# K's split turned in three products of sixteen rows per head, its diagonal tile filled by transfers that read each row twice, in an attention kernel on one Trainium2 core

## The chip, the core and the metric

The kernel runs on one core of a Trainium2 chip. Its engines are TensorE (PE: matrix products, with a row of its own, PEld, for loading weights), VectorE (DVE), ScalarE (ACT), GpSimd (POOL) and SyncE (SP). SP computes nothing here; it issues nearly all transfers, one after the other, and waits in between. The metric is the time of one execution on the device, in microseconds, of which the median of several runs is quoted.

## The reference

Cross attention with image tokens, for B = 16 sequences of S = 128 queries, C = 160 channels, H = 20 heads of D = 8. Each context has 124 text tokens and 4 image tokens of 256 features:

```python
q = heads(hidden_states @ W_q)
k_t = heads(text_ehs @ W_k);  v_t = heads(text_ehs @ W_v)
probs_t = softmax(einsum('bhsd,bhtd->bhst', q, k_t) * Dh ** -0.5)
text_out = einsum('bhst,bhtd->bhsd', probs_t, v_t)
k_ip = heads(ip_ehs @ W_k_ip);  v_ip = heads(ip_ehs @ W_v_ip)
attn_scores = einsum('bhsd,bhnd->bhsn', q, k_ip) * attn_scale
qsem = l2norm(einsum('bhst,bte->bhse', probs_t, text_ehs))
sem = einsum('bhse,bne->bhsn', qsem, l2norm(ip_ehs))
probs_ip = softmax(attn_scores + 0.5 * sem) * spatial_mask
ip_out = einsum('bhsn,bhnd->bhsd', probs_ip, v_ip)
out = (text_out + ip_out) @ W_out + b_out + residual
```

## The kernel before

**Windows and groups.** The program is a pipeline of 16 windows, one per sequence: four written out, ten in a loop of two at a time, two written out. A window has five groups (g = 0 to 4) of four heads. Every engine has its own list of instructions, in the order in which they are written, and semaphores tie them together. In window b, TensorE scores the groups of sequence b, turns the probabilities of two groups before (L934), multiplies those of three groups before with `main_rhs` (L952 and L954, called the mains here), and in between prepares sequence b + 1: at g = 0 the Gram matrix, V and K (L924) and q (L1024), at g = 1 the K products (L1031), at g = 2 the q products (L1039), at g = 4 the fifth group's (L1001, L1002). VectorE takes a maximum of each group's scores (L778) and norms of the mains (L713); ScalarE does the exponentials (L612), copies the turned probabilities to SBUF (L565) and makes the copies named below.

**The scores.** TensorE multiplies rounded float32 (fp32r) here. K and q are each split into a high part, written rounded by ScalarE (L581, L618), and the rest, written by VectorE (L784, L724). A head then has 32 columns: K as high, rest, high, rest and q as high, high, rest, rest, eight channels each, so that one product gives all four terms. Products with the identity turn four heads at a time into 128 rows. K's turned rows go from PSUM into `k_stack` (L600 for four groups, L591 for the fifth), and from there by transfers into `k_diag`, a tile that is zero but for its diagonal blocks: rows 32 j to 32 j + 31 of a group hold head j, in the columns of head j. With it one product of 512 columns (L984) scores four heads.

**The transfers of a window on SP** (L341 to L388), in this order: image-token rows of `k_split` for the next window, `ctxT_sb`, `xT_sb`, `xn_sb`, `vrep`; then, once `k_stack` is written, four transfers into `k_diag` for groups 0 to 3 (L373), one that repeats `g_stage` into `main_rhs` ten times (L378), once the fifth group's copies are made four more into `k_diag` (L383), and the store of a result (L388).

**`g_stage` is one buffer.** It holds the Gram matrix on its way to `main_rhs`, and ScalarE writes it at g = 0 only when the transfer of the window before has landed. In ScalarE's list the V copy, K's high part, that group's probabilities and everything later stand behind that write:

```python
wait(act, s_ctx_mm, b + 2)
wait(act, s_grep[p], 16 * (i + 1))
act.activation(g_stage[:, NIP:NIP + TOK], pa[:, 0:TOK], ACT.Copy)
```

The order of SP is fixed by lines 368 to 388; `s_kst03` counts L600 and `s_grep` the `main_rhs` transfers.

Of the kernel before, what the change touches and what calls it, by code (L numbers as in the profile page):

```python
# [24 lines left out]
F32 = mybir.dt.float32  # L25
F32R = mybir.dt.float32r
# [13 lines left out]
PG = HG // 2  # L40
NPAIR = H // 2
# [11 lines left out]
def xattn_program(nc, xT, xn, ctxT, ipT, ipn, smask, wq, wkv, wkvip, wout, ident, hmask, kip_d, vip_d, out):  # L53
    with ExitStack() as ctx:
# [48 lines left out]
        kip_split = sb("kip_split", [B * NIP, H, 2, 2, D])  # L103
# [72 lines left out]
        s_kd03 = two(sem, "s_kd03")  # L176
        s_kd4 = two(sem, "s_kd4")
# [28 lines left out]
        s_k0_mm = sem("s_k0_mm")  # L206
        s_k1_mm = sem("s_k1_mm")
# [106 lines left out]
        def _(sp):  # L314
# [17 lines left out]
            sp.dma_start(kip_d, kip_split[:, :, :, :, :].rearrange("t h c a d -> t (h c a d)")).then_inc(s_kip_out, 16)  # L332
# [7 lines left out]
            def window(b, p, i, w):  # L340
                n = 1 - p  # L341
                if has(w) and has(w, ahead=1) and w != 0:
# [4 lines left out]
                    wait(sp, s_kq4, b + 1)  # L347
                    sp.dma_start(k_split[T:TOK, :, :, :, :].rearrange("t h c a d -> t (h c a d)").bitcast(F32),
# [19 lines left out]
                if has(w, ahead=1):  # L368
# [160 lines left out]
        def _(act):  # L529
# [6 lines left out]
            act.activation(k_split[:, :, :, 0, :], doubled(probsT_ps[0][:, 0:C]), ACT.Copy).then_inc(s_khi, 1)  # L536
            act.wait_ge(s_q_mm, 1)
            act.activation(q_split[:, :, 0, :, :], doubled(probsT_ps[1][:, 0:C]), ACT.Copy).then_inc(s_qhi, 1)
            act.wait_ge(s_kT, 1)
            act.wait_ge(s_zeros[0], 1)  # L540
            for j in range(2):
                rows = slice(32 * j, 32 * j + 32)
                last = act.activation(k_diag[0][rows, 0:G - 1, j, :], pa[rows, :].rearrange("r (g t) -> r g t", t=TOK), ACT.Copy)
                if j == 0:
                    last.then_inc(s_kd03[0], 32)
                else:
                    last.then_inc(s_kst03, 1)
# [598 lines left out]
```

## Time and profile before

| | |
|---|---|
| median of 3 runs | 227.78 us (226.53 to 228.21) |
| profiled execution | 225.47 us, of which the span is 223.5 |
| TensorE busy | 210.6 us (94%), granted clock 0.992 |
| VectorE busy | 183.7 us (82%) |
| ScalarE busy | 172.7 us (77%) |
| GpSimd busy | 149.3 us (67%) |
| queue q1 (all of SP's transfers), share of 16 engines | 44.8% |

Durations come from the one profiled execution. Times in a row are counted from the start of its span. The profile lists a matrix product's own duration, though it overlaps its neighbours; what one adds is read from the chain of waits. "SPq" is SP's time for issuing a transfer, not the transfer; its landing is counted separately, from the start of the issue.

### The profile page before, as it was taken

How to read it: one execution, taken by the hardware profiler on the slowest of the kernel's cores; microseconds unless marked ns; L12 is line 12 of the kernel's file. 1: busy time of each engine (PE TensorE's matmuls, PEld its weight loads, DVE VectorE, ACT ScalarE, POOL GpSimd, SP SyncE). 2: the span in 40 equal slices, each digit the busy share in tenths (PEclk: the TensorE clock that was granted, in tenths of full speed). 3: DMA queues.
4: the chain of work that ended last, by engine and by line, in shares of the span. 5: the costliest groups of instructions: out<-in, count | busy, mean ns of one | idle time of the engine just before them, and what ended most of it. 6: DMA issues, size and time to landing. Idle time of an engine off the chain costs nothing.

```text
span 223.5 us, 6984 instructions
## 1 busy us (share of the span) xinstructions
PE 210.6 (94%) x1619; PEld 197.6 (88%) x1619; DVE 183.7 (82%) x1147; ACT 172.7 (77%) x569; POOL 149.3 (67%) x255
## 2 busy tenths in 40 slices
PE   8986859999999999999999999999999999998984
PEld 8876749999899999989999999999999999997973
DVE  4726529797988979697979899897979797999893
ACT  2608739897987979788888889697988888897831
POOL 2152301929688696959696977969696969698870
PEclk9996999999999999999999999999999999999999
DMA  5530553555462644565454647264545455461101
GB/s 137 110 121 18 115 148 72 146 142 155 128 164 70 193 112 124 147 158 149 135 155 121 181 103 198 76 181 109 153 123 158 148 144 149 105 167 32 47 1 44
DMA packets 47340, 27.60 MB, mean 123 GB/s; under 512 B 8513, under 2 KB 45538, under 8 KB 47322
## 3 DMA queue, kind: packets, MB, share of 16 engines
q1 hardware_dynamic: 46682, 26.96, 44.8%
q10 hardware_dynamic: 640, 0.43, 0.8%
q8 instruction: 7, 0.11, 0.2%
q14 instruction: 11, 0.09, 0.1%
HBM read 10.14 MB, written 1.52 MB: 52 GB/s over the span
## 4 chain that ended last, share of the span: by engine, by line
PE 68%; DVE 9%; DMA 8%; POOL 4%; issue 4%; ACT 3%; SPq 3%; DVEq 0%; POOLq 0%; ACTq 0%
PE main_ps L952 13%; PE main_ps L954 12%; PE probsT_ps L934 11%; DMA main_rhs<-g_stage 8%; PE pa L924 8%; PE score_ps L984 6%; PE pb L1012 4%; DVE junk L713 3%; PE pb L1024 3%; PE pa L1031 2%; PE main_ps L870 2%; PE pa L1039 2%; POOL rnorm L500 2%; SPq L373 1%; PE probsT_ps L865 1%
## 5 line engine op out<-in xcount | busy, mean ns | idle before, releaser
L612 ACT ACTIVATE probs<-score_ps,negmax 128x124 f32<-128x124 f32 x320 | 93.2, 411 | 1.1 <-DVE negmax L778 1.0
L713 DVE CUSTOM_DVE_ANT_0 junk<-main_ps,probs 128x124 f32<-128x124 f32 x320 | 77.8, 280 | 2.5 <-PE main_ps L954 2.0
L952 PE MATMUL main_ps<-main_rhs,probsT 124*128 124x137 f32 x320 | 64.8, 283 | 2.7 <-DVE small L715 2.7
L954 PE MATMUL main_ps<-main_rhs,probsT 124*128 124x137 f32 x320 | 63.3, 279 | 0.0
L500 POOL TENSOR_TENSOR rnorm<-clamped,exponent 128x20 f32<-128x20 f32 x15 | 53.2, 3544 | 1.2 <-DVE clamped L698 1.2
L778 DVE TENSOR_REDUCE negmax<-score_ps 128x4 f32<-128x496 f32 x80 | 53.1, 663 | 0.0
L952 PEld LDWEIGHTS main_ps<-main_rhs,probsT 124*128 124x128 f32 x320 | 48.9, 190 | 4.5 <-ACT probsT L565 2.0
L565 ACT ACTIVATE probsT<-probsT_ps 124x512 f32<-124x512 f32 x80 | 50.9, 636 | 2.5 <-PE probsT_ps L934 1.7
L934 PE MATMUL probsT_ps<-ident_sb,probs 128*124 128x128 f32 x320 | 49.0, 276 | 0.0
L954 PEld LDWEIGHTS main_ps<-main_rhs,probsT 124*128 124x128 f32 x320 | 48.7, 188 | 0.0
L934 PEld LDWEIGHTS probsT_ps<-ident_sb,probs 128*124 128x124 f32 x320 | 39.1, 141 | 5.3 <-issue 0.4
L984 PE MATMUL score_ps<-k_diag,q_stack 128*128 128x512 f32 x80 | 39.1, 489 | 1.0 <-DMA k_diag<-k_stack 1.0
L777 DVE COPY ip_score<-score_ps 128x16 f32<-128x16 f32 x80 | 13.3, 166 | 19.5 <-PE score_ps L984 19.5
L715 DVE COPY small<-main_ps 128x26 f32<-128x26 f32 x160 | 28.8, 180 | 0.1
L713 DVE DVE_READ_ACCUMULATOR2_ANT norm<- 128x1 f32 x320 | 26.6, 83 | 0.0
L478 POOL TENSOR_TENSOR ip_exp_half<-ip_exp 128x40 f32<-128x40 f32 x14 | 3.5, 252 | 25.1 <-ACT ip_exp L606 25.1
L576 ACT ACTIVATE g_stage<-pa 128x128 f32<-128x128 f32 x15 | 4.2, 278 | 20.5 <-DMA main_rhs<-g_stage 13.5
L303 POOL TENSOR_TENSOR ip_prod<-vrep,ip_probs 128x640 f32<-128x640 f32 x13 | 18.2, 1403 | 0.0
L924 PE MATMUL pa<-wkv_sb,ctxT_sb 128*128 128x160 f32 x112 | 17.5, 299 | 0.0
L984 PEld LDWEIGHTS score_ps<-k_diag,q_stack 128*128 128x128 f32 x80 | 15.4, 193 | 1.2 <-DMA k_diag<-k_stack 1.2
L600 ACT ACTIVATE k_stack<-pa 128x512 f32<-128x512 f32 x15 | 9.0, 598 | 9.4 <-PE pa L1031 9.3
L924 PEld LDWEIGHTS pa<-wkv_sb,ctxT_sb 128*128 128x128 f32 x112 | 15.7, 190 | 0.0
(165 smaller groups left out, 343.5 us busy)
## 6 DMA issues: line engine op xcount, KB each, us to landing
main_rhs<-g_stage SPq DMA_DIRECT2D x16, 660.0 KB, 4.2
vrep<-vip_d SPq DMA_DIRECT2D x13, 320.0 KB, 3.6
k_diag<-k_stack SPq DMA_DIRECT2D x60, 64.0 KB, 2.2
ctxT_sb<-ctxT SPq DMA_DIRECT2D x16, 124.0 KB, 2.7
xT_sb<-xT SPq DMA_DIRECT2D x16, 80.0 KB, 2.1
xn_sb<-xn SPq DMA_DIRECT2D x15, 80.0 KB, 2.0
out<-out_sb SPq DMA_DIRECT2D x15, 80.0 KB, 1.7
k_diag<-k_stack SPq DMA_DIRECT2D x60, 16.0 KB, 1.8
```

Source lines behind the costliest of these rows:

```text
L303: eng.tensor_tensor(ip_prod[:, :, :, :], vrep[n][:, :, :, :], ip_probs[:, :, :].rearrange("s h m -> s m h").unsqueeze(3).broadcast_to([S, ...
L500: pool.tensor_tensor(rnorm[:, :], clamped[:, :], exponent[:, :], ALU.pow).then_inc(s_rnorm, 1)
L565: act.activation(probsT[tp][:, :, :].rearrange("t h s -> t (h s)"), probsT_ps[tp][0:T, :], ACT.Copy).then_inc(s_probsT, 1)
L612: last = act.activation(probs[p][:, h, :], score_ps[(p * G + g) % 2][:, j * TOK:j * TOK + T], ACT.Exp, bias=negmax[p][:, h:h + 1])
L713: dve.tensor_tensor_reduce(junk[:, 2 * r + a, :], u, probs[wb][:, h, :], 1.0, 0.0, ALU.mult, ALU.add, norm2[wb][:, h:h + 1])
L715: dve.tensor_copy(small[wb][:, PG * gg + r, :], main_ps[r][:, T:T + SMALL]).then_inc(s_norm, 1)
L778: dve.tensor_reduce(negmax[p][:, HG * g:HG * g + HG], sc[:, :, 0:T], AX_X, ALU.max, negate=True).then_inc(s_max, 1)
L924: mm = pe.matmul(pa[:, lo:lo + width], ctxT_sb[n][:, c, :], r, start=(c == 0), stop=(c == EC - 1))
L934: mm = pe.transpose(probsT_ps[tp][0:T, j * S:(j + 1) * S], probs[tb][:, HG * tg + j, :], ident_sb[:, :])
L952: pe.matmul(main_ps[r][:, 0:MAIN], probsT[mp][:, 2 * r, :], blk[:, RW - MAIN:RW], start=True, stop=True)
L954: pe.matmul(main_ps[r][:, MAIN:2 * MAIN], probsT[mp][:, 2 * r + 1, :], blk[:, 0:MAIN], start=True, stop=True).then_inc(s_main, 1)
L984: pe.matmul(score_ps[(p * G + g) % 2][:, :], q_stack[p][:, g, :], k_diag[p][:, g, :, :].rearrange("r h t -> r (h t)"), start=True, stop=Tr ...
```

## The change

K's split is no longer doubled. `k_split` holds 16 columns per head (channel, then high or rest), `q_split` 32 in a matching order (channel, K's part, q's part). So K's 20 heads are turned in three products, eight heads in each of two and four in the third, all at g = 1; the fifth K product at g = 4 goes, and with it a `k_stack` copy on ScalarE. Even groups come out in rows 0 to 63 of `k_stack`, odd ones in rows 64 to 127. The doubling is done by the transfers into `k_diag`: each reads 16 rows twice into 32. `k_diag` is laid out with the block first, and even groups (slots 0 to 2) before odd ones (3 and 4), so a row of a transfer is one piece of 1536 or 1024 bytes instead of several of 512. Four transfers fill the even groups and signal `s_kd_even`, four the odd ones, `s_kd_odd`; all eight now stand before the `main_rhs` transfer. Window 0 has a K tile and semaphores of its own. The loop's parts of the diff:

```diff
--- before.py
+++ after.py
@@ -38,6 +38,7 @@
 HG = 4
 G = H // HG
 PG = HG // 2
+KT = (G + 1) // 2
 NPAIR = H // 2
 PARTED = (0, 3, 4, 5)
 TAIL = 3
...
@@ -109,11 +110,12 @@
 
         g_stage = sb("g_stage", [TOK, NIP + TOK])
         v_stage = sb("v_stage", [T, C])
-        k_split = sb("k_split", [TOK, H, 2, 2, D], F32R)
-        q_split = sb("q_split", [S, H, 2, 2, D], F32R)
-        k_stack = sb("k_stack", [128, G, TOK])
+        k0_split = sb("k0_split", [TOK, H, D, 2, 2], F32R)
+        k_split = sb("k_split", [TOK, H, D, 2], F32R)
+        q_split = sb("q_split", [S, H, D, 2, 2], F32R)
+        k_stack = sb("k_stack", [128, KT, TOK])
         q_stack = two(sb, "q_stack", [128, G, S], F32R)
-        k_diag = two(sb, "k_diag", [128, G, HG, TOK], F32R)
+        k_diag = two(sb, "k_diag", [128, HG, G, TOK], F32R)
         main_rhs = two(sb, "main_rhs", [TOK, NPAIR, RW])
 
         negmax = two(sb, "negmax", [S, H])
@@ -173,8 +175,8 @@
         s_vrep_in = two(sem, "s_vrep_in")
         s_kip_in = sem("s_kip_in")
         s_grep = two(sem, "s_grep")
-        s_kd03 = two(sem, "s_kd03")
-        s_kd4 = two(sem, "s_kd4")
+        s_kd_even = two(sem, "s_kd_even")
+        s_kd_odd = two(sem, "s_kd_odd")
         s_store = two(sem, "s_store")
 
         s_hmask_in = sem("s_hmask_in")
...
@@ -268,7 +272,15 @@
         def doubled(cols):
 
             r = cols.rearrange("t (h d) -> t h d", d=D)
-            return r.unsqueeze(2).broadcast_to([r.shape[0], H, 2, D])
+            return r.unsqueeze(3).broadcast_to([r.shape[0], H, D, 2])
+
+        def by_head(cols):
+
+            return cols.rearrange("t (h d) -> t h d", d=D)
+
+        def slot(g):
+
+            return g // 2 + KT * (g % 2)
 
         def windows(eng, window):
 
...
@@ -344,8 +356,7 @@
                     if w == 1:
                         sp.wait_ge(s_kip_out, 16)
                     wait(sp, s_kT, b + 1)
-                    wait(sp, s_kq4, b + 1)
-                    sp.dma_start(k_split[T:TOK, :, :, :, :].rearrange("t h c a d -> t (h c a d)").bitcast(F32),
+                    sp.dma_start(k_split[T:TOK, :, :, :].rearrange("t h d a -> t (h d a)").bitcast(F32),
                                  kip_d[bass.ds((b + 1) * NIP, NIP), :]).then_inc(s_kip_in, 16)
                 if has(w) and has(w, ahead=2):
 
@@ -369,19 +380,17 @@
 
                     wait(sp, s_scores, G * b)
                     wait(sp, s_kst03, b + 2)
-                    for j in range(HG):
-                        sp.dma_start(k_diag[n][32 * j:32 * j + 32, 0:G - 1, j, :].bitcast(F32),
-                                     k_stack[32 * j:32 * j + 32, 0:G - 1, :]).then_inc(s_kd03[n], 16)
+                    for odd in range(2):
+                        for j in range(HG):
+                            lo = 64 * odd + 16 * j
+                            sp.dma_start(k_diag[n][32 * j:32 * j + 32, j, KT * odd:KT + (G - KT) * odd, :].bitcast(F32),
+                                         k_stack[lo:lo + 16, 0:KT - odd, :].unsqueeze(1).broadcast_to(
+                                             [16, 2, KT - odd, TOK])).then_inc((s_kd_even, s_kd_odd)[odd][n], 16)
 
                     wait(sp, s_main, NPAIR * b)
                     wait(sp, s_gstage, b + 2)
                     sp.dma_start(main_rhs[n][:, :, D + 1:D + 1 + NIP + TOK],
                                  g_stage[:, :].unsqueeze(1).broadcast_to([TOK, NPAIR, NIP + TOK])).then_inc(s_grep[n], 16)
-
-                    wait(sp, s_st4, b + 2)
-                    for j in range(HG):
-                        sp.dma_start(k_diag[n][32 * j:32 * j + 32, G - 1, j, :].bitcast(F32),
-                                     k_stack[32 * j:32 * j + 32, G - 1, :]).then_inc(s_kd4[n], 16)
                 if has(w, lag=3):
 
                     wait(sp, s_final, b - 2)
...
@@ -578,7 +587,7 @@
                         wait(act, s_vcopy, b + 1)
                         act.activation(v_stage[:, :], pa[0:T, TOK:TOK + C], ACT.Copy)
                         kr = TOK if w == 0 else T
-                        act.activation(k_split[0:kr, :, :, 0, :], doubled(pa[0:kr, TOK + C:TOK + 2 * C]),
+                        act.activation(k_split[0:kr, :, :, 0], by_head(pa[0:kr, TOK + C:TOK + 2 * C]),
                                        ACT.Copy).then_inc(s_khi, 1)
                     if g == 3 and has(w) and has(w, ahead=1):
 
@@ -588,16 +597,15 @@
                     if g == 4 and has(w) and has(w, ahead=1):
 
                         wait(act, s_kq4, b + 2)
-                        act.activation(k_stack[:, G - 1, :], pb[:, 0:TOK], ACT.Copy)
                         act.activation(q_stack[n][:, G - 1, :], pb[:, TOK:TOK + S], ACT.Copy).then_inc(s_st4, 1)
                     if has_group(w, g, 2):
                         transposed(grp - 2, (p * G + g) % 2)
                     if g == 1 and has(w, ahead=1):
 
                         wait(act, s_kT, b + 2)
-                        wait(act, s_kd03[p], 64 * (i + 1))
-                        wait(act, s_kd4[p], 64 * (i + 1))
-                        act.activation(k_stack[:, 0:G - 1, :].rearrange("r g t -> r (g t)"), pa[:, :],
+                        wait(act, s_kd_even[p], 64 * (i + p))
+                        wait(act, s_kd_odd[p], 64 * (i + p))
+                        act.activation(k_stack[:, :, :].rearrange("r k t -> r (k t)"), pa[:, 0:KT * TOK],
                                        ACT.Copy).then_inc(s_kst03, 1)
                     if g == 2 and has(w, lag=2):
 
@@ -615,7 +623,7 @@
                     if g == 0 and has(w, ahead=1):
 
                         wait(act, s_q_mm, b + 2)
-                        act.activation(q_split[:, :, 0, :, :], doubled(pb[:, 0:C]),
+                        act.activation(q_split[:, :, :, :, 0], doubled(pb[:, 0:C]),
                                        ACT.Copy).then_inc(s_qhi, 1)
 
             windows(act, window)
...
@@ -721,8 +729,8 @@
                     if g == 2 and has(w, ahead=1):
 
                         wait(dve, s_qhi, b + 2)
-                        dve.tensor_tensor(q_split[:, :, 1, :, :], doubled(pb[:, 0:C]),
-                                          q_split[:, :, 0, :, :], ALU.subtract).then_inc(s_qlo, 1)
+                        dve.tensor_tensor(q_split[:, :, :, :, 1], doubled(pb[:, 0:C]),
+                                          q_split[:, :, :, :, 0], ALU.subtract).then_inc(s_qlo, 1)
                     if g == 3 and has(w, lag=3):
 
                         wait(dve, s_ipout, 3 * (b - 2))
...
@@ -781,8 +789,8 @@
 
                         wait(dve, s_khi, b + 2)
                         kr = TOK if w == 0 else T
-                        dve.tensor_tensor(k_split[0:kr, :, :, 1, :], doubled(pa[0:kr, TOK + C:TOK + 2 * C]),
-                                          k_split[0:kr, :, :, 0, :], ALU.subtract).then_inc(s_klo, 1)
+                        dve.tensor_tensor(k_split[0:kr, :, :, 1], by_head(pa[0:kr, TOK + C:TOK + 2 * C]),
+                                          k_split[0:kr, :, :, 0], ALU.subtract).then_inc(s_klo, 1)
             windows(dve, window)
 
             tiles = (tail_guard, tail_rden, tail_clamped)
@@ -857,7 +865,7 @@
 
             def stacked(split, g):
 
-                return split[:, HG * g:HG * g + HG, :, :, :].rearrange("t h a b d -> t (h a b d)")
+                return split[:, HG * g:HG * g + HG, :, :, :].rearrange("t h d a c -> t (h d a c)")
 
             def project(dst, n, rhs, first, last):
 
...
@@ -976,13 +985,17 @@
                         if w == 0 and g == 2:
                             pe.wait_ge(s_v0, 1)
                         if g == 0:
-                            wait(pe, s_kd03[p], 64 * (i + 1))
+                            if w == 0:
+                                pe.wait_ge(s_kd0_03, 64)
+                            wait(pe, s_kd_even[p], 64 * (i + p))
                             wait(pe, s_qst03, b + 1)
-                        if g == G - 1:
-                            wait(pe, s_kd4[p], 64 * (i + 1))
+                        if g == 1:
+                            wait(pe, s_kd_odd[p], 64 * (i + p))
+                        if g == 3 and w == 0:
+                            pe.wait_ge(s_kd0_4, 64)
                         wait(pe, s_exp, grp - 1)
                         pe.matmul(score_ps[(p * G + g) % 2][:, :], q_stack[p][:, g, :],
-                                  k_diag[p][:, g, :, :].rearrange("r h t -> r (h t)"), start=True,
+                                  k_diag[p][:, :, slot(g), :], start=True,
                                   stop=True).then_inc(s_scores, 1)
                     if g == 0 and w == 0:
                         pe.wait_ge(s_ctx_in[1], 16)
@@ -998,7 +1011,6 @@
 
                         wait(pe, s_final, b - 2)
                         wait(pe, s_qlo, b + 2)
-                        pe.matmul(pb[:, 0:TOK], stacked(k_split, G - 1), ident_r_sb[:, :], start=True, stop=True)
                         pe.matmul(pb[:, TOK:TOK + S], stacked(q_split, G - 1), ident_r_sb[:, :], start=True,
                                   stop=True).then_inc(s_kq4, 1)
                     if has_group(w, g, 2):
...
@@ -1027,8 +1039,9 @@
 
                         wait(pe, s_klo, b + 2)
                         wait(pe, s_kip_in, 16 * b)
-                        for k in range(G - 1):
-                            mm = pe.matmul(pa[:, k * TOK:(k + 1) * TOK], stacked(k_split, k), ident_r_sb[:, :],
+                        for k in range(KT):
+                            heads = k_split[:, 2 * HG * k:min(2 * HG * (k + 1), H), :, :].rearrange("t h d a -> t (h d a)")
+                            mm = pe.matmul(pa[0:heads.shape[1], k * TOK:(k + 1) * TOK], heads, ident_r_sb[:, :],
                                            start=True, stop=True)
                         mm.then_inc(s_kT, 1)
                     if g == 2 and has(w, ahead=1):
...
```

SP in the loop, from `vrep` on, before (`REGISTER_ALU` and `ISA` rows set up register values and addresses):

```order
L365 DMA vrep<-vip_d 128x640
L295 REGISTER_ALU
L373 DMA k_diag<-k_stack 32x4x128 x4
L295 REGISTER_ALU
L378 DMA main_rhs<-g_stage 128x10x132
L383 DMA k_diag<-k_stack 32x128 x4
L388 ISA
L388 DMA out<-out_sb 128x160
```

and the same stretch of the change:

```order
L376 DMA vrep<-vip_d 128x640
L307 REGISTER_ALU
L386 DMA k_diag<-k_stack 32x1x384 x4
L386 DMA k_diag<-k_stack 32x1x256 x4
L307 REGISTER_ALU
L392 DMA main_rhs<-g_stage 128x10x132
L397 ISA
L397 DMA out<-out_sb 128x160
```

The second four transfers into `k_diag` have moved ahead of the one into `main_rhs`.

TensorE at g = 4 of a window, before:

```order
L954 MATMUL main_ps<-main_rhs,probsT 128x137
L984 MATMUL score_ps<-k_diag,q_stack 128x512
L1001 MATMUL pb<-ident_r_sb,k_split 128x128
L1002 MATMUL pb<-ident_r_sb,q_split 128x128
L934 MATMUL probsT_ps<-ident_sb,probs 124x128 x4
L952 MATMUL main_ps<-main_rhs,probsT 128x137
```

and of the change, from the K products at g = 1 to the next group's probabilities:

```order
L963 MATMUL main_ps<-main_rhs,probsT 128x137
L1044 MATMUL pa<-ident_r_sb,k_split 128x128 x2
L1044 MATMUL pa<-ident_r_sb,k_split 64x128
L997 MATMUL score_ps<-k_diag,q_stack 128x512
L943 MATMUL probsT_ps<-ident_sb,probs 124x128 x4
```

The four K products before (`L1031 MATMUL pa<-ident_r_sb,k_split 128x128 x4`) have become three, and L1001 has no counterpart.

## Rows read from the trace of the kernel before

**Rows 1.** The page, part 4: the chain that ended last, share by engine.

```profile
PE 68%; DVE 9%; DMA 8%; POOL 4%; issue 4%; ACT 3%; SPq 3%; DVEq 0%; POOLq 0%; ACTq 0%
```

**Rows 2.** Stretches: length, busy us (instructions) of each engine, granted clock, DMA share, GB/s.

```profile
31.80:43.26 11.46, 9.62 (x79) 9.13 (x78) 9.54 (x65) 10.16 (x35) 4.61 (x5) 1.00 0.41 109
116.38:128.41 12.03, 12.03 (x98) 11.52 (x97) 10.85 (x70) 10.43 (x36) 9.58 (x17) 1.00 0.52 143
188.71:223.50 34.79, 30.24 (x227) 27.12 (x225) 29.52 (x194) 22.48 (x71) 23.52 (x33) 1.00 0.24 65
```

**Rows 3.** Timeline of ScalarE, early: start, length, instruction, idle time before it and releaser.

```profile
31.80 0.28 ACT L576 ACTIVATE g_stage<-pa 128x128 f32<-128x128 f32 x1 [5.08 <-DMA main_rhs<-g_stage]
...
43.26 0.28 ACT L576 ACTIVATE g_stage<-pa 128x128 f32<-128x128 f32 x1 [0.76 <-DMA main_rhs<-g_stage]
...
46.91 0.60 ACT L600 ACTIVATE k_stack<-pa 128x512 f32<-128x512 f32 x1 [0.47 <-PE pa L1031]
...
55.32 0.28 ACT L576 ACTIVATE g_stage<-pa 128x128 f32<-128x128 f32 x1 [1.29 <-DMA main_rhs<-g_stage]
```

**Rows 4.** Timeline of SP's queue in the same windows.

```profile
27.57 0.67 SPq L378 DMA_DIRECT2D main_rhs<-g_stage  x1
...
47.58 2.59 SPq L373 DMA_DIRECT2D k_diag<-k_stack  x4
50.26 0.66 SPq L378 DMA_DIRECT2D main_rhs<-g_stage  x1
```

**Rows 5.** Lines L373, L383, L378: issue ns min/median/max; issue to landing, L373, then L378.

```profile
L373 SPq DMA_DIRECT2D k_diag<-k_stack x60: 595/604/1446, 24.8 to 195.8; - x60
...
DMA to landing us min/median/max: 2.0/2.2/3.2
...
L383 SPq DMA_DIRECT2D k_diag<-k_stack x60: 543/591/1324, 28.3 to 200.4; - x60
...
DMA to landing us min/median/max: 4.1/4.2/5.0
```

**Rows 6.** Timelines of VectorE and TensorE, window 2, and of TensorE, window 14.

```profile
44.16 0.49 DVE L784 TENSOR_TENSOR k_split<-pa,k_split 124x320 fp32r<-124x320 f32 x1 [0.57 <-ACT k_split L581]
...
45.30 0.47 PE L952 MATMUL main_ps<-main_rhs,probsT 124*128 124x137 f32 x2
...
191.32 0.40 PE L952 MATMUL main_ps<-main_rhs,probsT 124*128 124x137 f32 x2
```

**Rows 7.** Timeline of SP's queue, a steady window.

```profile
109.10 2.60 SPq L373 DMA_DIRECT2D k_diag<-k_stack  x4
111.87 0.67 SPq L378 DMA_DIRECT2D main_rhs<-g_stage  x1
```

**Rows 8.** Timeline of ScalarE, the same window and the start of the next.

```profile
104.27 0.28 ACT L576 ACTIVATE g_stage<-pa 128x128 f32<-128x128 f32 x1 [0.77 <-PE pa L924]
...
108.42 0.60 ACT L600 ACTIVATE k_stack<-pa 128x512 f32<-128x512 f32 x1 [0.65 <-PE pa L1031]
...
116.38 0.28 ACT L576 ACTIVATE g_stage<-pa 128x128 f32<-128x128 f32 x1 [0.84 <-PE pa L924]
```

**Rows 9.** The chain in order of time: start us, us in the chain, what.

```profile
107.99 0.40 PE pa L1031 x4
...
113.16 0.06 PE pb L1001
...
116.27 0.23 PE score_ps L984
```

**Rows 10.** Groups of instructions by line and form: busy us, mean ns, idle time before.

```profile
L581 ACT ACTIVATE k_split<-pa 124x320 fp32r<-124x320 f32 x14 | 6.4, 457 | 0.0
L579 ACT ACTIVATE v_stage<-pa 124x160 f32<-124x160 f32 x15 | 4.7, 311 | 0.0
L731 DVE TENSOR_TENSOR attn_out<-ip_out,text 128x160 f32<-128x160 f32 x13 | 4.4, 335 | 0.0
```

**Rows 11.** Timeline of SP's queue: the issue that reads image-token rows from HBM.

```profile
105.15 0.28 SPq L348 DMA_DIRECT2D k_split<-kip_d  x1
```

More of the change, by code:

```diff
@@ L206, in xattn_program @@
         s_k0_mm = sem("s_k0_mm")
+        s_kd0_03 = sem("s_kd0_03")
+        s_kd0_4 = sem("s_kd0_4")
         s_k1_mm = sem("s_k1_mm")
@@ L535, in _ @@
             act.wait_ge(s_k0_mm, 1)
-            act.activation(k_split[:, :, :, 0, :], doubled(probsT_ps[0][:, 0:C]), ACT.Copy).then_inc(s_khi, 1)
+            act.activation(k0_split[:, :, :, 0, :], doubled(probsT_ps[0][:, 0:C]), ACT.Copy).then_inc(s_khi, 1)
             act.wait_ge(s_q_mm, 1)
-            act.activation(q_split[:, :, 0, :, :], doubled(probsT_ps[1][:, 0:C]), ACT.Copy).then_inc(s_qhi, 1)
+            act.activation(q_split[:, :, :, :, 0], doubled(probsT_ps[1][:, 0:C]), ACT.Copy).then_inc(s_qhi, 1)
             act.wait_ge(s_kT, 1)
@@ L542, in _ @@
                 rows = slice(32 * j, 32 * j + 32)
-                last = act.activation(k_diag[0][rows, 0:G - 1, j, :], pa[rows, :].rearrange("r (g t) -> r g t", t=TOK), ACT.Copy)
+                last = act.activation(k_diag[0][rows, j, 0:G - 1, :], pa[rows, :].rearrange("r (g t) -> r g t", t=TOK), ACT.Copy)
                 if j == 0:
-                    last.then_inc(s_kd03[0], 32)
+                    last.then_inc(s_kd0_03, 32)
                 else:
@@ L550, in _ @@
                 rows = slice(32 * j, 32 * j + 32)
-                act.activation(k_diag[0][rows, G - 1, j, :], pb[rows, 0:TOK], ACT.Copy).then_inc(s_kd4[0], 16)
+                act.activation(k_diag[0][rows, j, G - 1, :], pb[rows, 0:TOK], ACT.Copy).then_inc(s_kd0_4, 16)
             act.wait_ge(s_qT, 1)
@@ L660, in _ @@
             dve.wait_ge(s_khi, 1)
-            dve.tensor_tensor(k_split[:, :, :, 1, :], doubled(probsT_ps[0][:, 0:C]), k_split[:, :, :, 0, :],
+            dve.tensor_tensor(k0_split[:, :, :, 1, :], doubled(probsT_ps[0][:, 0:C]), k0_split[:, :, :, 0, :],
                               ALU.subtract).then_inc(s_klo, 1)
             dve.wait_ge(s_qhi, 1)
-            dve.tensor_tensor(q_split[:, :, 1, :, :], doubled(probsT_ps[1][:, 0:C]), q_split[:, :, 0, :, :],
+            dve.tensor_tensor(q_split[:, :, :, :, 1], doubled(probsT_ps[1][:, 0:C]), q_split[:, :, :, :, 0],
                               ALU.subtract).then_inc(s_qlo, 1)
@@ L671, in _ @@
                 rows = slice(32 * j, 32 * j + 32)
-                dve.tensor_copy(k_diag[0][rows, 0:G - 1, j, :],
-                                pa[rows, :].rearrange("r (g t) -> r g t", t=TOK)).then_inc(s_kd03[0], 16)
+                dve.tensor_copy(k_diag[0][rows, j, 0:G - 1, :],
+                                pa[rows, :].rearrange("r (g t) -> r g t", t=TOK)).then_inc(s_kd0_03, 16)
             dve.wait_ge(s_kq4, 1)
@@ L676, in _ @@
                 rows = slice(32 * j, 32 * j + 32)
-                dve.tensor_copy(k_diag[0][rows, G - 1, j, :], pb[rows, 0:TOK]).then_inc(s_kd4[0], 16)
+                dve.tensor_copy(k_diag[0][rows, j, G - 1, :], pb[rows, 0:TOK]).then_inc(s_kd0_4, 16)
             dve.wait_ge(s_ipunit_T, 1)
@@ L885, in _ @@
             for k in range(G - 1):
-                mm = pe.matmul(pa[:, k * TOK:(k + 1) * TOK], stacked(k_split, k), ident_r_sb[:, :], start=True, stop=True)
+                mm = pe.matmul(pa[:, k * TOK:(k + 1) * TOK], stacked(k0_split, (0, 2, 4, 1)[k]), ident_r_sb[:, :], start=True,
+                               stop=True)
             mm.then_inc(s_kT, 1)
-            pe.matmul(pb[:, 0:TOK], stacked(k_split, G - 1), ident_r_sb[:, :], start=True, stop=True)
+            pe.matmul(pb[:, 0:TOK], stacked(k0_split, 3), ident_r_sb[:, :], start=True, stop=True)
             pe.wait_ge(s_qlo, 1)
@@ L1000, in window @@
                         wait(pe, s_qlo, b + 2)
-                        pe.matmul(pb[:, 0:TOK], stacked(k_split, G - 1), ident_r_sb[:, :], start=True, stop=True)
                         pe.matmul(pb[:, TOK:TOK + S], stacked(q_split, G - 1), ident_r_sb[:, :], start=True,
@@ L1018, in window @@
                         if w == 0:
-                            pe.wait_ge(s_kd4[0], 64)
+                            pe.wait_ge(s_kd0_4, 64)
                         wait(pe, s_xT_in[n], 16 * (i + p + 1))
```

16 lines of the change are left out of this document (8 added, 8 removed).

## The prediction

> **What bounds the kernel now.** I read the chain of waits first, then one steady window on each engine, then the early windows, because they behave differently. The chain puts 68% of the span on TensorE, and 8% on the transfer that copies `g_stage` into `main_rhs` [rows 1]. Busy time by stretch splits the two regimes [rows 2]: from 116.38 to 128.41 us TensorE is busy for all 12.03 us, so a steady window is TensorE's work and nothing else. From 31.80 to 43.26 it is busy for only 9.62 of 11.46 us, and the granted clock is 1.00 all the same.
>
> What sets that early window is a loop through three engines and the DMA queue. ScalarE may write `g_stage` for the next window only when the last `main_rhs<-g_stage` transfer has landed. In window 0 the transfer is issued at 27.57, and ScalarE, idle for 5.08 us, writes at 31.80 [rows 3, 4]. In window 2 the whole circle can be read: `g_stage` at 43.26, `k_stack` at 46.91 (3.65 later), SP's first `k_diag` issue at 47.58 (0.67), the `main_rhs` issue at 50.26 (2.68), the next `g_stage` at 55.32 (5.06). That is 12.06 us. The last step is the transfer; over all windows its landing is 4.1 to 5.0 us behind its issue, median 4.2 [rows 5].
>
> The 3.65 us are a path too. VectorE stands idle for 0.57 us until ScalarE has written the first half of K's split, then subtracts for the second half at 44.16. The norms are queued behind that, and the mains of the second group wait for them and start at 45.30. The K products come next, and ScalarE's `k_stack` copy waits for these [rows 3, 6].
>
> In a steady window the same loop runs just under TensorE: issue at 111.87, so landing at about 116.1, and `g_stage` at 116.38, which waited for TensorE. That is a margin of 0.3 us here; ScalarE's other idle time in the loop is the 0.65 us before `k_stack` at 108.42 [rows 7, 8]. **So the order in which SP issues its transfers is nearly critical before anything is changed.**
>
> **The change, part by part.**
>
> *TensorE.* The fifth K product goes, and the first four become three, the last with 64 of 128 stationary columns. Four take 0.40 us in the chain, so one takes 0.10; the one at L1001 takes 0.06, its weights being loaded under the score product before it [rows 9]. The q product behind it then takes that place, so up to a full 0.10 is saved. The narrower third saves at most half of its 0.10. The ends are 0.16 and 0.25; I take 0.22 per window, 15 windows, 3.3 us, if TensorE stays the bound. A steady window would be 12.03 - 0.22 = 11.8.
>
> *ScalarE and VectorE.* K's halves are written once, 160 columns instead of 320. The nearest rows of 160 columns give 311 ns against 457 on ScalarE, and 335 on VectorE against 0.49 us [rows 6, 10], 0.15 us each, both on the 3.65 us path. With the one K product less (0.10) that step becomes 3.25. ScalarE's own queue has a floor near it: from `g_stage` at 104.27 to `k_stack` at 108.42 less 0.65 idle is 3.50, less 0.15 is 3.35 [rows 8]. I take 3.3. The `k_stack` copy shrinks from 512 to 384 columns: with 0.28 us for 128 and 0.60 for 512 [rows 8] that is 0.11 less, so SP starts 0.56 after instead of 0.67. The fifth `k_stack` copy goes as well, but ScalarE is not the bound there: nothing.
>
> *Strided writes.* Both splits are now written 8 bytes apart. No row shows such a write. It costs nothing at the low end, and at the high end doubles the element time, by the rows of the loop's two K writes: 0.15 more on each engine, 0.3 us per window. I take nothing: the K write of before already leaves out every other 32 bytes, and its 0.46 us is hardly more than the 0.44 that the contiguous copies' rate gives for 320 columns [rows 8, 10]. The 0.3 is kept for the range. The Trainium skill ("SBUF — State Buffer", "Door 1: The DMA port swizzle") says that fp32 may be strided by up to 4 elements free, within a 16-byte line; by that rule the cost is nil, and no run here shows it.
>
> *Transfers.* Each window issued 4 + 1 + 4: four of 64 KB, the `main_rhs` transfer, four of 16 KB. Now it is 8 + 1, and the `main_rhs` transfer stands behind all eight. Same bytes, fewer and longer packets. What SP's time for an issue depends on decides everything. Four of the large take 2.60 us, 0.65 apart, of which 0.60 is the issue [rows 7, 5]. The small ones carry a quarter of the packets, 32 rows against 128, and take 0.59 [rows 5]. **The issue therefore does not follow packets or bytes.** The new ones keep 32 destination rows in SBUF and a source in SBUF, so I take 0.65 apart; the cheapest issue of a window, with its source in HBM, is 0.28 [rows 11], the dearest of `k_diag` was 1.45 [rows 5]; these are the ends. Eight take 5.2, and with the 0.1 before the next issue 5.3, where 2.68 stood.
>
> The Trainium skill ("DMA: Bandwidth & Descriptors", "Issuing engines are not separate DMA queues") says that the sequencer's time to initiate a DMA is "usually small relative to the DMA itself". For a single transfer that holds here, 0.60 against a landing of 2.2 us; for eight in a row it does not. By the rule the move costs nothing and the sum is TensorE's 3.3 us gain.
>
> *New waits.* The even groups are wanted at the next window's first score, 7.9 us behind `k_stack` (108.42 to 116.27) [rows 8, 9]. Their last issue is over 0.56 + 2.6 = 3.2 behind it, and lands 2.2 later [rows 5]: hidden, by 2.5. The odd ones land 8.0 behind it and are wanted a group later, a fifth of 12.03 us, so at 10.3: hidden, by 2.3. Were this cover gone, TensorE itself would stop at the score. The wait for the fourth group's product goes. The transfer for `k_split`'s image rows no longer waits for the fourth group's copies, and SP's queue behind `main_rhs` gets no longer: nothing.
>
> **The sum.** The loop becomes 3.3 + 0.56 + 5.3 + 4.25 (median landing and a handover) = 13.4 us. TensorE needs 11.8, so the loop now bounds every window; TensorE, ScalarE and VectorE wait in it. Window 1's `g_stage` was at 31.80; four more issues put it 2.6 later, and the two image-token copies that SP waits for in window 0 are shorter by about 0.3, so 34.1. Thirteen loops of 13.4 bring the last `g_stage` to 208.3, against 188.71 [rows 2]: +19.6. Behind it stood 34.79 us. TensorE is further ahead when the wait ends (in the waiting window 2 the mains of the second group start 2.04 behind `g_stage`, in the last window, where nothing waits, 2.61 [rows 3, 6]: 0.6), and with two shorter steps 0.4 more: -1.0. Together +18.6 on the profiled execution's 225.47, which is 244.1. The median of the runs shown is 227.78, 2.3 above it: **246.4 us**, I say 246.
>
> **Rivals.**
>
> *A, the issues get cheap.* With contiguous rows of 1536 bytes an issue could fall towards 0.28. The loop equals TensorE's 11.8 at 3.6 us for eight, 0.45 apart; below that the kernel is faster: 227.78 - 3.3 = 224.5. For it: issues differ by shape from 0.28 to 0.67 [rows 7, 11]. Against it: a quarter of the packets saved 0.01. Chance 0.11.
>
> *B, the order of the issues does not matter*: SP works ahead of the transfers, so that `main_rhs` lands when the bytes in front of it are through, and these are the same. Also 224.5. Against it: the landing follows the issue by 4.1 to 5.0 in all windows, and SP starts on `k_diag` only when `k_stack` is done, so it has nothing to work ahead on. Chance 0.05. The rule of the Trainium skill cited above would bring this about.
>
> *C, no change.* The saved products give nothing, or issues of about 0.47 give back just the gain: 227.8. Chance 0.04.
>
> *D, slower still.* The landing is 5.0, as behind 50.26, in most windows, since the issues for the next window's inputs now follow it at once, or the strided writes cost their 0.3: 0.8 or 0.3 us times 13 loops, so 257 or 250, 261 with both. For it: the 5.06 of window 2. Against it: the median of 4.2. Chance 0.11.
>
> *Forecast*, 0.69: 246, itself 237 to 254 (issues 0.60 to 0.70 apart, 0.05 x 8 x 13 = 5 us; the rest landing and the 3.3).
>
> The range takes in a part of D and of partly cheaper issues: 234 to 258. About 1% is what a measurement of this kernel can tell from no change. Faster 0.16, same 0.04, slower 0.80.
>
> **What would show it.** In the changed profile: eight `k_diag` issues in a row, about 5.2 us; ScalarE waiting for the `main_rhs` transfer before `g_stage` in all 15 windows, over 20 us in total; TensorE idle in each window, and windows of 13.4 us. The forecast is wrong if the issues are 0.45 us apart or less, or if `g_stage` waits for TensorE in steady windows.

## The result, and the profile after

| | before | changed |
|---|---|---|
| median | 227.68 us (226.53 to 228.21, 4 runs) | 248.98 us (248.73 to 250.89, 4 runs) |
| ratio of changed to before | | 1.099, 95% interval 1.094 to 1.104 |
| profiled execution, span | 225.47, 223.5 | 248.73, 246.7 |

The kernel is 21.3 us slower. The forecast was 246 us with a range of 234 to 258. Medians here and below are over all runs of a kernel; the ratios leave out two runs, one of each of the two kernels under "Constants later", that took over 1.5% longer than the fastest of the same kernel.

The chain of waits of the changed kernel, shares of the span by engine, which answers [rows 1]:

```profile
DMA 26%; DVE 25%; PE 23%; issue 9%; ACT 6%; SPq 6%; POOL 3%; DVEq 1%; ACTq 0%; POOLq 0%
DMA main_rhs<-g_stage 26%; DVE junk L721 8%; PE main_ps L961 5%; PE main_ps L963 4%; PE pb L1024 4%; SPq L386 4%; DVE norm L721 3%; PE probsT_ps L943 3%; DVE negmax L786 3%; DVE small L723 3%; ACT k_split L590 2%; DVE oT L778 2%; PE main_ps L878 2%; PE score_ps L997 2%; POOL rnorm L509 1%
```

TensorE's 68% is down to 23%, and one transfer, `main_rhs<-g_stage`, carries 26% instead of 8%. Who waited for whom, with total us, number of times and the longest:

```profile
ACT g_stage L585 <- DMA main_rhs<-g_stage: 47.7, 15, 8.3
...
DVE k_split L792 <- ACT k_split L590: 32.2, 15, 4.9
...
PE main_ps L961 <- DVE small L723: 16.5, 15, 4.1
```

It is one wait, seen three times. ScalarE waits for the landing in all 15 windows (before it was 6 windows and 13.5 us), VectorE for ScalarE's high part of K, and TensorE for the norms that are queued behind VectorE's rest. TensorE's own row names VectorE, which is not at fault.

One circle of the loop in a steady window, ScalarE's timeline first, then SP's, a later stretch of time than in [rows 7, 8]:

```profile
119.06 0.28 ACT L585 ACTIVATE g_stage<-pa 128x128 f32<-128x128 f32 x1 [2.40 <-DMA main_rhs<-g_stage]
...
122.38 0.49 ACT L608 ACTIVATE k_stack<-pa 128x384 f32<-128x384 f32 x1 [0.26 <-PE pa L1044]
...
132.38 0.28 ACT L585 ACTIVATE g_stage<-pa 128x128 f32<-128x128 f32 x1 [2.45 <-DMA main_rhs<-g_stage]
```

```profile
122.96 5.09 SPq L386 DMA_DIRECT2D k_diag<-k_stack  x8
128.22 0.65 SPq L392 DMA_DIRECT2D main_rhs<-g_stage  x1
```

From `g_stage` to `k_stack` 3.32 us, to SP's first issue 0.58, to the `main_rhs` issue 5.26, to the next `g_stage` 4.16: 13.32 us, where 13.4 was forecast as 3.3 + 0.56 + 5.3 + 4.25. The line of the `k_diag` issues, duration in ns, and below it their time from issue to landing, to set beside [rows 5]:

```profile
L386 SPq DMA_DIRECT2D k_diag<-k_stack x120: 578/592/1121, 24.8 to 220.5; - x120
...
DMA to landing us min/median/max: 1.9/2.1/3.1
```

A row of a transfer is 1536 or 1024 bytes long instead of several of 512, and the issue still takes 592 ns, where it took 604 and 591. The landing moved by 0.1 us, from 2.2 to 2.1.

### The profile page after: what moved, and what is told of

Read it like the earlier page. It is cut to its first block, busy times and chain, and to the rows that moved or that the text cites. A ratio compares the mean times of both kernels' runs of the same rounds, so it can differ in the third digit from the quotient of the medians.

```text
span 246.7 us, 6905 instructions
## 1 busy us (share of the span) xinstructions
PE 217.4 (88%) x1589; PEld 197.3 (80%) x1589; DVE 181.5 (74%) x1147; ACT 168.1 (68%) x554; POOL 149.2 (60%) x255
## 3 DMA queue, kind: packets, MB, share of 16 engines
HBM read 10.06 MB, written 1.43 MB: 47 GB/s over the span
## 4 chain that ended last, share of the span: by engine, by line
DMA 26%; DVE 25%; PE 23%; issue 9%; ACT 6%; SPq 6%; POOL 3%; DVEq 1%; ACTq 0%; POOLq 0%
DMA main_rhs<-g_stage 26%; DVE junk L721 8%; PE main_ps L961 5%; PE main_ps L963 4%; PE pb L1024 4%; SPq L386 4%; DVE norm L721 3%; PE probsT_ps L943 3%; DVE negmax L786 3%; DVE small L723 3%; ACT k_split L590 2%; DVE oT L778 2%; PE main_ps L878 2%; PE score_ps L997 2%; POOL rnorm L509 1%
## 5 line engine op out<-in xcount | busy, mean ns | idle before, releaser
L620 ACT ACTIVATE probs<-score_ps,negmax 128x124 f32<-128x124 f32 x320 | 92.2, 397 | 1.7 <-DVE negmax L786 1.4
L961 PE MATMUL main_ps<-main_rhs,probsT 124*128 124x137 f32 x320 | 68.6, 296 | 17.0 <-DVE small L723 16.5
L961 PEld LDWEIGHTS main_ps<-main_rhs,probsT 124*128 124x128 f32 x320 | 49.6, 193 | 24.1 <-DVE small L723 11.8
L963 PE MATMUL main_ps<-main_rhs,probsT 124*128 124x137 f32 x320 | 64.3, 283 | 0.0
L963 PEld LDWEIGHTS main_ps<-main_rhs,probsT 124*128 124x128 f32 x320 | 49.8, 192 | 0.0
L943 PEld LDWEIGHTS probsT_ps<-ident_sb,probs 128*124 128x124 f32 x320 | 39.6, 142 | 6.3 <-issue 0.7
L997 PE MATMUL score_ps<-k_diag,q_stack 128*128 128x512 f32 x80 | 39.7, 497 | 1.3 <-DMA k_diag<-k_stack 1.0
L792 DVE TENSOR_TENSOR k_split<-pa,k_split 124x160 fp32r<-124x160 f32 (+1 forms) x15 | 4.9, 325 | 32.2 <-ACT k_split L590 32.2
L785 DVE COPY ip_score<-score_ps 128x16 f32<-128x16 f32 x80 | 13.3, 167 | 20.0 <-PE score_ps L997 20.0
```

The source lines that it names most:

```text
L620: last = act.activation(probs[p][:, h, :], score_ps[(p * G + g) % 2][:, j * TOK:j * TOK + T], ACT.Exp, bias=negmax[p][:, h:h + 1])
L943: mm = pe.transpose(probsT_ps[tp][0:T, j * S:(j + 1) * S], probs[tb][:, HG * tg + j, :], ident_sb[:, :])
L961: pe.matmul(main_ps[r][:, 0:MAIN], probsT[mp][:, 2 * r, :], blk[:, RW - MAIN:RW], start=True, stop=True)
L963: pe.matmul(main_ps[r][:, MAIN:2 * MAIN], probsT[mp][:, 2 * r + 1, :], blk[:, 0:MAIN], start=True, stop=True).then_inc(s_main, 1)
L997: pe.matmul(score_ps[(p * G + g) % 2][:, :], q_stack[p][:, g, :], k_diag[p][:, :, slot(g), :], start=True, stop=True).then_inc(s_scores, 1)
```

## The experiments

Each was run beside the kernel before on the same chip (226.4 to 227.1 us there), and the ratios are to that. Times of different experiments come from different chips, so differences of a microsecond between them say little.

**The order alone.** The changed kernel with `main_rhs` between the even and the odd four:

```diff
-                    for odd in range(2):
-                        for j in range(HG): ... # k_diag, even, then odd
+                    for j in range(HG): ...     # k_diag, even
                     wait(sp, s_main, NPAIR * b)
                     wait(sp, s_gstage, b + 2)
                     sp.dma_start(main_rhs[n]..., g_stage...).then_inc(s_grep[n], 16)
+                    for j in range(HG): ...     # k_diag, odd
```

> The changed kernel with SP's order alone altered: the main_rhs transfer is issued between the four even and the four odd k_diag transfers instead of behind all eight. Theory (the loop over g_stage is set by how many issues stand ahead of main_rhs): four issues and their 2.6 us leave the loop, 13.30 - 2.6 = 10.7 us, below TensorE's 11.8, so steady windows become TensorE's and the time is 224 to 226 us, a little faster than before. The odd k_diag issues then end 6.7 us behind k_stack, land at 8.8, and are wanted at about 10.2: no new wait. Rival 1 (the loss comes from the layout, the strided writes or the double reading, and not from the order): stays at 245 to 249. Rival 2 (both): in between, 230 to 240.

Measured 224.34 us, ratio 0.988 (0.981 to 0.995). Everything else of the change is in it, and it is 1.2% faster than before. Its steady windows alternate between 11.74 and 11.95 us, and in them `g_stage` waits for TensorE again. Rival 1, the layout or the strided writes as the cause, falls: the order of nine issues is worth 24.6 us (248.98 less 224.34).

One thing did not go as expected. TensorE waits for `k_diag` five times, 5.3 us in all, where the kernel before waits once, 1.0 us; the four new waits (1.56, 0.53, 0.94 and 1.24 us) lie in windows 1 to 3 and in the last. The four odd issues, which now stand directly behind `main_rhs`, take 3.44 us instead of 2.5, and they land 3.0 us behind their issue instead of 2.0.

**Extra issues in the kernel before.**

```diff
+                    for j in range(HG):
+                        sp.dma_start(spare[32 * j:32 * j + 32, :], k_stack[32 * j:32 * j + 32, 0, :]).then_inc(s_kd03[n], 16)
                     wait(sp, s_main, NPAIR * b)
```

> The kernel before with four more small transfers (16 KB each, k_stack to a spare tile) issued between the four k_diag transfers and the main_rhs one; nothing else changes, and nothing reads the spare tile. Theory: 4 x 0.61 = 2.5 us join the loop, 11.0 + 2.5 = 13.5 to 13.8 us per window against 12.05, so 245 to 252 us, and ScalarE waits for main_rhs before g_stage in all windows. Rival (the changed kernel's loss belongs to its layout and products): 228 to 230, since the transfer engines are less than half busy.

Measured 257.24 us, ratio 1.135 (1.128 to 1.142), above the 245 to 252 expected. SP's queue, and ScalarE's wait, there:

```profile
124.85 2.59 SPq L374 DMA_DIRECT2D k_diag<-k_stack  x4
127.49 2.50 SPq L377 DMA_DIRECT2D spare<-k_stack  x4
130.16 0.67 SPq L381 DMA_DIRECT2D main_rhs<-g_stage  x1
```

```profile
ACT g_stage L579 <- DMA main_rhs<-g_stage: 47.9, 15, 7.0
```

The loop that starts at 120.55 takes 13.82 us, the upper end of what was expected, but every other one takes 13.98 and the early ones up to 15.04; the mean of 13 is 14.09. One side effect is in it: the signal that the first score of a window waits for counts the spare transfers too, and TensorE waited for them until 31.65 (2.87 us) and 46.59 (1.14 us) and once in the last window, but not in a steady one. Sixty-four KB more per window, with no new data, no new layout and no new product, bring the whole loss and more. So the mechanism does not need any of this change's other parts; it is in the kernel before, kept off by 0.3 us.

**The loop cut open.** The changed kernel, order untouched:

```diff
-        g_stage = sb("g_stage", [TOK, NIP + TOK])
+        g_stage = two(sb, "g_stage", [TOK, NIP + TOK])
...
-                        wait(act, s_grep[p], 16 * (i + 1))
+                        wait(act, s_grep[n], 16 * (i + p))
```

The new wait is for the transfer of two windows ago, and `g_stage[n]` is written and sent in place of `g_stage`.

> The changed kernel, its SP order untouched (main_rhs behind all eight k_diag transfers), but with two g_stage tiles in turn, so that ScalarE waits for the main_rhs transfer of two windows ago. Theory: the loop is cut open, nothing waits for the landing, and the time is TensorE's: 223 to 226 us. Rival 1 (late main_rhs or k_diag data hold TensorE itself): 235 to 247, with TensorE waiting for a transfer. Rival 2 (SP's total issue time is the bound): 240 and up, since SP's work is unchanged.

Measured 221.75 us, ratio 0.976 (0.969 to 0.983); once more in another call, 221.07, ratio 0.975 (0.972 to 0.978). A stretch of one window (its length, then busy us of TensorE, its loads, VectorE, ScalarE and GpSimd, then the granted clock, the DMA share and GB/s):

```profile
114.27:126.11 11.84, 11.84 (x97) 11.28 (x96) 10.60 (x70) 10.22 (x35) 9.66 (x16) 1.00 0.56 145
```

TensorE is busy all of it, with the eight issues still ahead of `main_rhs`:

```profile
118.89 5.09 SPq L386 DMA_DIRECT2D k_diag<-k_stack  x8
124.16 0.66 SPq L392 DMA_DIRECT2D main_rhs<-g_stage  x1
```

In a steady window a late `main_rhs` hurts nobody but the writer of `g_stage`. Rivals 1 and 2 of this experiment fall.

**Issues or bytes.** The changed kernel with one group in each transfer (`KT * odd:KT * odd + 1` and `0:1` for the slots), so 128 KB ahead of `main_rhs` instead of 320. The kernel leaves the other groups with old K; it serves for its time alone.

> The changed kernel with every one of the eight k_diag transfers carrying one group only (16 KB), so groups 2 to 4 keep old K data and the output is not the reference's; the same eight issues in the same place. Theory (issues, not bytes or packets, make the loop longer): 5.1 us for eight issues again and 247 to 249 us. Rival (the transfers' bytes in front of main_rhs delay it): 40% of the bytes, so the landing moves forward by up to 0.5 us per window and the time falls to about 242.

Measured 248.66 us, ratio 1.098 (1.091 to 1.105), as with all the bytes (1.099). In the same place:

```profile
122.23 5.08 SPq L386 DMA_DIRECT2D k_diag<-k_stack  x8
127.49 0.65 SPq L392 DMA_DIRECT2D main_rhs<-g_stage  x1
```

**Six ahead.** The changed kernel with the odd transfers split, two ahead of `main_rhs` and two behind.

> The changed kernel with six k_diag transfers (four even, two odd) ahead of main_rhs and two behind it. Theory (each issue ahead of main_rhs adds its 0.65 us to the loop): 13.30 - 1.30 = 12.0 us per window, just over TensorE's 11.83; 13 loops of 1.3 us less than 249 are 232 us. Rival (a fixed price of having the odd transfers ahead, whatever their number): 245 to 249. Rival 2 (another step binds at about 12.7): 238 to 242.

Measured 233.92 us, ratio 1.031 (1.026 to 1.035). ScalarE and SP in one window:

```profile
122.82 0.28 ACT L595 ACTIVATE g_stage<-pa 128x128 f32<-128x128 f32 x1 [1.64 <-DMA main_rhs<-g_stage]
...
126.12 0.49 ACT L618 ACTIVATE k_stack<-pa 128x384 f32<-128x384 f32 x1 [0.26 <-PE pa L1054]
...
135.05 0.28 ACT L595 ACTIVATE g_stage<-pa 128x128 f32<-128x128 f32 x1 [1.36 <-DMA main_rhs<-g_stage]
```

```profile
126.69 2.51 SPq L385 DMA_DIRECT2D k_diag<-k_stack  x4
129.25 1.23 SPq L390 DMA_DIRECT2D k_diag<-k_stack  x2
130.65 0.66 SPq L396 DMA_DIRECT2D main_rhs<-g_stage  x1
```

The issues give back the 1.30 us foreseen (3.96 instead of 5.26). The window is 12.23 and not 12.0, since the landing is 4.40 instead of 4.16. The next window is 12.49: there the step from `g_stage` to `k_stack` is 3.50, and why is open. Two more `k_diag` issues follow `main_rhs` directly here, which may be why it lands later. The guess was not tested by itself, but the medians of the other traces agree with it: 4.3 us where four follow directly (the order alone, and the two cuts together below), 4.1 or 4.2 where none does.

Those two issues take much longer than the ones ahead:

```profile
131.35 2.10 SPq L401 DMA_DIRECT2D k_diag<-k_stack  x2
```

That is 1.05 us each, against 0.63 for the same kind ahead of `main_rhs`. So bytes and packets do not set the time of a `k_diag` issue here, but what stands directly before it can.

With four, six and eight ahead the time is 224.3, 233.9 and 249.0. With four TensorE bounds; between six and eight an issue costs 7.5 us, near 0.65 x 13 = 8.5.

**The two cuts together, and the tiles in the kernel before.**

> The changed kernel with both edits: main_rhs issued between the even and the odd k_diag transfers, and two g_stage tiles in turn. Theory (with the loop cut open SP's order matters no more): the same as with two tiles alone, 221 to 223 us. Rival (a late main_rhs still costs something, for instance through GpSimd or the last window): 1 to 3 us less than with two tiles alone, 219 to 220. Rival 2 (the odd k_diag transfers, now a transfer later, are waited for): 223 to 226.

> The kernel before with two g_stage tiles in turn and nothing else. Its steady windows are TensorE's already, so they stay at 12.05 us; only the waits of the windows 1 to 6 go. Theory: 225 us, and the difference to the changed kernel with two tiles (221.75) is the gain of the K products alone, 3 to 3.5 us (0.22 per window). Rival (the gain there came from the tiles, not from the products): 222.

Together 222.57 us, ratio 0.982 (0.977 to 0.987): no better than two tiles alone, as expected once the loop is open. Rival 2 is in the trace all the same: TensorE waits for `k_diag` four times, 4.8 us in all, against once and 1.0 with the tiles alone.

The tiles in the kernel before: 222.85, ratio 0.981 (0.978 to 0.985). The theory had 225, its rival 222, and the rival came: most of what the changed kernel gains with two tiles comes from the tiles, not from the products. The steady window of this kernel, to compare with the 11.84 above:

```profile
113.95:126.06 12.11, 12.11 (x99) 11.57 (x98) 10.85 (x70) 10.43 (x36) 9.68 (x17) 1.00 0.51 142
```

So a window gains 0.27 us from the products (0.22 forecast), which would be 3.5 us in 13 windows, but the whole kernels differ by only 1.1 us (222.85 and 221.75, on different chips). The windows' times say where it goes: from window 1's `g_stage` to window 2's it is 16.74 us with the change and 13.84 without. What TensorE waited for around there, with the change and two tiles:

```profile
27.95 0.51 PE L997 MATMUL score_ps<-k_diag,q_stack 128*128 128x512 f32 x1 [1.02 <-DMA k_diag<-k_stack]
...
34.63 0.47 PE L1044 MATMUL pa<-ident_r_sb,k_split 128*128 128x128 f32 x3 [2.38 <-DMA k_split<-kip_d]
```

The first wait is hardly new: the kernel before has it too (0.97 us), and with two tiles 1.40. The second is 0.74 us without the change. It does not come from a late issue: the image-token rows of `k_split` are issued at 29.78, against 32.08 without the change, but TensorE goes on 4.85 us behind that issue instead of 1.97. With the change they stand directly behind the `main_rhs` transfer, issued at 29.00 and landed 5.3 us later; without it four small transfers lie between. That they land so late for that reason is likely, not tested. The clock takes the rest: behind the wait of 2.38 us the granted clock reads 0.50 from 36.60 to 39.00, and the window's mean is 0.90 against 1.00 without the change. Of the 2.9 us, 1.6 are longer busy time of TensorE (13.36 against 11.74) and 1.3 idle time.

The next experiment was built on another reading, that SP is late in window 1 because it begins with constants.

**Constants later.** The changed kernel with two tiles, and three loads moved into an idle stretch of SP in window 1 (beside it the two tiles alone, once more):

```diff
-            sp.dma_start(smask_sb...); sp.dma_start(wout_sb...); sp.dma_start(hmask_sb...)
...
                     sp.dma_start(xT_sb[p][:, :, :], xT[b + 2]).then_inc(s_xT_in[p], 16)
+                    if w == 1: # the three loads
```

> The changed kernel with two g_stage tiles, and three constant loads (about 1.9 us of SP's issue time) moved from ahead of window 0's k_diag transfers to an idle stretch of SP in window 1. With the loop cut open, window 1 still took 16.7 us against 13.8 in the kernel before with two tiles, because TensorE waited 1.0 us for k_diag and 2.4 us for k_split's image rows, which SP issues behind eight k_diag transfers. Theory (issue order again): everything that SP issues in window 0 comes 1.9 us sooner, TensorE's two waits shrink, and the time is 1.5 to 2 us below two tiles alone, 220. Rival (GpSimd, which waits for one of the constants, holds window 1 up instead): the same 221 to 222 or more.

> The changed kernel with two g_stage tiles once more, on the same chip as the run with the constants later, for the comparison: 221 to 222.5 us.

Measured 220.09 us, ratio 0.971 (0.967 to 0.976), the fastest of all, against 221.07 beside it; the profiled spans are 217.7 and 219.6. TensorE's waits did not shrink as I had it, they are 1.43 and 2.40 (0.97 and 2.37 beside it); all of it comes 1.4 us sooner (`g_stage` at 25.17 instead of 26.61), and the next window's `g_stage` sooner still (40.66 against 43.26). That second gain, 1.2 us, is the clock: it stayed at 1.00 in this window, where it averaged 0.90 beside it, and TensorE was busy for 11.69 us instead of 13.33. The wait before it was the same, 2.40 and 2.37 us, so this part of the gain may be chance and the edit need not bring it again. The intervals of the two ratios overlap, so of the kernel's own gain only the sign is likely; that it beats the kernel before is clear.

**The clock in window 1.** The changed kernel with its four transposes repeated (`for j in tuple(range(HG)) * 8`, in window 1, group 1 only).

> The changed kernel with TensorE's four transposes of window 1, group 1 done eight times over (the same values into the same bank), which fills most of the 4.1 us for which it waits there. Question: window 1's loop is 16.33 us where 13.4 was forecast, and the step from g_stage to k_stack is 4.63 instead of 3.3, while the granted clock reads 0.68. Theory (the clock fell to its lower level behind the idle stretch): the clock stays at 1.00, the step is 3.2 to 3.4 us, the time falls by about 1.3. Rival (VectorE's or ScalarE's first pass is slow there, whatever the clock): the step stays at 4.6.

Measured 247.82 us, one run. In the changed kernel TensorE idled for 4.13 us, until 36.47, and from there to 39.10 the granted clock read 0.50. Over the step from `g_stage` to `k_stack` it averaged 0.68; kept busy, it read 1.00. First the row of the changed kernel, then those of this one, with its next window:

```profile
34.47:39.10 4.63, 2.63 (x12) 2.67 (x13) 3.44 (x22) 3.05 (x12) 0.00 (x0) 0.68 0.02 6
```

```profile
34.37:37.82 3.45, 2.38 (x21) 2.17 (x20) 2.57 (x15) 3.06 (x12) 0.00 (x0) 1.00 0.02 7
48.72:53.10 4.38, 2.63 (x12) 2.66 (x13) 3.36 (x23) 3.05 (x11) 0.33 (x1) 0.70 0.34 93
```

The step from `g_stage` to `k_stack` falls from 4.63 to 3.45 us. In both TensorE first waits 2.0 us of it for the norms; what follows takes 2.63 us at the lower clock and 1.45 at the full one, so the clock was the cause. A window later, where TensorE was not kept busy and idled for 2.76 us, the clock falls to 0.70 and the step is 4.38. The fall is put off, not removed.

## Why the prediction was right

- **The bound and its margin.** The 0.3 us of slack behind `main_rhs` was real: eight issues ahead use it up, and so do four spare ones in the kernel before.
- **The price of an issue.** Taken as 0.65 apart, since transfers with a quarter of the packets took as long; measured 5.09 for eight, 0.64. The run with 40% of the bytes settles it: 5.08. Rival A (cheap issues) falls with this, and rival B (the order does not matter) with the experiment on the order. The rule of the Trainium skill ("DMA: Bandwidth & Descriptors", "Issuing engines are not separate DMA queues"), that the time to initiate a DMA is usually small relative to the DMA, does not carry over to eight in a row: 5.09 us of issuing stand against 2.1 from one issue to its landing. Rival D (slower landings) did not come: the median is 4.1.
- **The loop.** 13.32 against 13.4, each of four steps within 0.1 us.
- **Products.** 0.22 per window forecast, 0.27 measured once the loop is open (12.11 to 11.84). In the changed kernel itself none of it shows, and with two tiles window 1 takes most of it back.
- **K written once.** ScalarE's high part takes 339 ns and VectorE's rest 326, against 311 and 335 assumed; the step they belong to came out at 3.32 against 3.3.
- **Strided writes.** The range had 0.3 us for them, and they cost nothing that can be seen. VectorE's write of q's rest went from 482 to 483 ns. ScalarE's of the high part went from 494 to 525, but the stride is not the reason: with the same layout and two tiles it is 493, and with the old layout and four more transfers 504. The Trainium skill ("SBUF — State Buffer", "Door 1: The DMA port swizzle") says that fp32 may be strided by up to 4 elements free, and these rows agree. Whether K's 339 ns, against 312 for the V copy of the same size, have any of it is not shown.
- **New waits.** Hidden in steady windows. For the rows of `k_split` the prediction had nothing; once the longer wait was gone, TensorE waited 2.4 us for them in window 1. I had worked out cover from a steady window only, and had not asked what stands directly ahead of them in the queue. The wait of 1.0 us for `k_diag` there is not new.
- **The mis-sized terms.** The sum was 2.6 us low, as the net of two errors. The last `g_stage` was at 212.27 and not 208.3: window 1 took 16.33 us, 2.9 over the forecast loop, of which 1.3 is the clock's fall and 1.7 a landing of 5.98. Windows 2 to 5 took 1.4 too much: in window 2 the clock fell once more, behind 3.47 us of idle time, and the step to `k_stack` took 3.77; in windows 3 to 5 the `k_diag` issues took 5.59 to 5.80 instead of 5.3. The eight later windows took 0.7 too little together, and the start was 0.4 late. The tail was 34.4, not 33.8. Against these 4.6 us stood 2.1: the median lay 0.25 above the profiled execution, and not 2.3 as before. That this cancelled half of the error was luck; for the profiled execution itself the sum gave 244.1, and it took 248.73.

Why the landing in window 1 took 5.98 us stays open; with fewer bytes the same one took 4.90, with other kernels 4.28 to 5.1.

## What to carry to other kernels

Count a queue's issues, not its bytes: here a `k_diag` issue costs 0.64 us in the line of whatever stands behind it, and 1.05 directly behind the 660 KB transfer; merging rows into longer pieces saved none of that. Before moving a transfer, find who waits for its landing and for what reason; a wait for a buffer to be free closes a loop over all engines, whose length can be added up from four rows, and a second buffer of 528 bytes per partition opens it. Check the cover for a moved transfer in the first windows too, and look at what it comes to stand directly behind.

## What the runs showed of the hardware

**The clock.** In the changed kernel TensorE idled for 4.13 us, and from 36.47 to 39.10 the granted clock read 0.50, the level of 1.2 GHz. This cost 1.2 us beside the idle time itself. Behind 3.47 us a window later it averaged 0.66 over the next 2.0. Behind 2.38 us, in the changed kernel with two tiles, it read 0.50 from 36.60 to 39.00. Behind 2.40 us, with the constants later, and behind 1.84 in the kernel before it stayed at 1.00, the level of 2.4 GHz. The length of the one idle stretch therefore does not decide alone. In steady windows of 13.3 us with 0.8 us idle the clock stayed at 1.00.

**The queue directly behind a large transfer.** What follows the 660 KB transfer into `main_rhs` at once is slower than elsewhere, in issue and in landing. An issue of `k_diag` takes 1.05 us there and 0.64 ahead of it. The issue of `k_split`'s image rows has a median of 796 ns in the changed kernel, where no `k_diag` transfer lies between, and 289 ns in the run with both cuts, where four do. The store of the result lands 3.5 us behind its issue in the changed kernel, and 1.7 in the kernel before and with the order alone, where four `k_diag` transfers lie between. None of this is on the changed kernel's loop in a steady window.
